# Attention and routed experts on one core: the early tiles' Newton steps on GpSimd, and four operations of the hand-over placed later

## The chip, the cores and the metric

One core of one Trainium2 chip runs the whole program. The metric is the device time of one execution in microseconds, the median over the runs shown. Less is better. Engines are named as in the profile: PE is TensorE, PEld its weight loads, DVE is VectorE, ACT is ScalarE, POOL is GpSimd, SP is SyncE, which here issues most of the transfers.

## The reference

All in float32, for 32 batches of 64 tokens of 512 features (2048 tokens, 16 tiles of 128):

```python
x = x + tanh(g_xattn) * attention(layernorm(x), ctx)       # 32 heads of 128, 4 key/value heads, 128 keys
x = x + tanh(g_ffn) * ffn(layernorm(x))
# ffn, with xt the 2048 normed tokens:
scores = softmax(xt @ router_w + router_b) + router_bias   # 16 experts in 4 groups
# keep the best 2 groups by their maximum, then the best 2 experts; gate = their scores
y = sum over experts of gate * ((silu(xt @ w1 + b1) * (xt @ w2 + b2)) @ w3 + b3)
z = (silu(xt @ sw1 + sb1) * (xt @ sw2 + sb2)) @ sw3 + sb3  # the shared expert, inner width 256
return y + z
```

The layernorm divides by the square root of variance + 1e-5.

## The kernel before, in words

Precision: nearly every product is done as three passes over operands split into a rounded part and a rest (`three_pass`, L82 to L86): hi times hi, lo times hi, hi times lo. So each operand of TensorE is first copied by ScalarE (the hi part) and then subtracted by VectorE (the lo part). `y` in SBUF holds all 16 tiles of the running x.

Stage one makes keys and values. Stage two (`stage_two`) is the attention. It runs 128 steps m (a batch of one key/value head each), and each engine walks the same steps in its own function `step` (ScalarE L810, VectorE L901, TensorE L1036). The order on each engine is written out by hand; semaphores connect them. In step m TensorE makes the scores `ps_s`, turns the previous step's probabilities (`ps_p`), projects queries for a later step (`ps_q`, not in the last four steps), multiplies the probabilities with the values (`ps_o`, which needs VectorE's `p_lo`), and does half of an output product into the one bank `ps_y` (heads 4 to 7 in even steps, 0 to 3 in odd ones, L1012). ScalarE copies half of the scores out (`s_cross`), VectorE adds the other half (`s_sb`, L908), takes the maximum (`nmax`), splits the turned probabilities (`p_lo`), and so on. Every second step VectorE adds a finished tile from `ps_y` into `y` (`add_pair`, L888), and before the next output product starts anew in `ps_y` TensorE waits for that addition (`added`). In the step after an addition VectorE takes the tile's statistics (`moments`, L894). Three more steps (128 to 130) drain the pipeline.

The second norm, its transposes and the router (`SecondNorm`) start inside the last steps. Tiles 0 to 8 are round 0, tiles 9 to 11 round 1, tiles 12 to 15 round 2. For rounds 0 and 1, `inverse_root` (L524 to L541) runs on VectorE at the end of steps 120 and 125: one addition of epsilon, a shift and a subtraction for the first guess, then three Newton iterations of four instructions, each waiting for the one before. Round 2 uses ScalarE's square root after the last addition (L1642). GpSimd norms tiles 0 to 11 and 15 (`normalise`, L561), VectorE tiles 12 to 14. TensorE turns the normed tiles in steps 124 to 128 (`turn`, L574: two, three, three, three, one tile) and the last four after the drain; ScalarE and VectorE split the result into `x_hi` (L582) and `x_lo` (L587). `logits(pe, o, ...)` (L599, L601) makes the router's products of octet o (four tiles, 512 tokens), `copy_logits` (L608) copies them out, and `turn_logits` (L613) turns them to tokens on partitions.

The hooks `act_extra`, `dve_extra` and `pe_extra` (L1466 to L1500) put further operations at the end of a given step: the split of the first shared half's weights (ScalarE step 125, L1120; VectorE step 126, L1155), the copy of the logits of octets 0 and 1 (steps 129, 130) and the router products of octets 0 and 1 (steps 128, 129).

After the drain the routing follows: a chain on VectorE from the logits (L1780) to the choice of experts (`mask`, L1812), then ranks on TensorE (L1968, L1970), slots, and the gathered expert work. The bias rows of the experts (`bias_rows`, `b3`, L1765 and L1768) are split between the last x_lo and the routing. In the trace the tiles `hot_row`/`b` of these lines are `b3_raw` and `b3`, and `w_raw<-bank` and `rows_in<-bank` at L608 are the logits' copies. The last output product of step 130 is followed on TensorE by octet 2's router products, the turned logits of octets 0 and 1, the turns of tiles 12 to 15, octet 3's products, and the first shared half's up products.

Of the kernel before, what the change touches and what calls it, by code (L numbers as in the profile page):

```python
# [22 lines left out]
ACT = mybir.ActivationFunctionType  # L23
# [462 lines left out]
class SecondNorm:  # L486
# [5 lines left out]
    def __init__(self, b, common, signals, normed, x_hi, x_lo, rw, logits_t, roots, banks, fold, bias_copied):  # L492
# [19 lines left out]
        self.roots_made = 0  # L512
# [6 lines left out]
    def inverse_root(self, dve, k):  # L519
# [4 lines left out]
        def then(ins):  # L524
            self.roots_made += 1
            ins.then_inc(self.rooted, 1)
            dve.wait_ge(self.rooted, self.roots_made)

        whole = mybir.dt.uint32
        then(dve.tensor_scalar(v, self.mean_var[:, lo:hi, 1], EPS, None, ALU.add))  # L530
        then(dve.tensor_scalar(w.bitcast(whole), v.bitcast(whole), 1, None, ALU.logical_shift_right))
        then(dve.tensor_scalar(r.bitcast(whole), w.bitcast(whole), -1.0, float(0x5f3759df), ALU.mult, ALU.add))
        for i in range(3):
            then(dve.tensor_tensor(w, r, r, ALU.mult))
            then(dve.tensor_tensor(w, w, v, ALU.mult))
            then(dve.tensor_scalar(w, w, -0.5, 1.5, ALU.mult, ALU.add))
            out = self.rstd[:, lo:hi] if i == 2 else r
            last = dve.tensor_tensor(out, r, w, ALU.mult)  # L538
            if i < 2:
                then(last)  # L540
        last.then_inc(self.rstd_made, 1)  # L541

# [75 lines left out]
def stage_two(nc, a, common, scratch):  # L618
# [4 lines left out]
    with ExitStack() as stack:  # L623
# [236 lines left out]
        def vector(dve):  # L860
# [40 lines left out]
            def step(s, o, g):  # L901
# [41 lines left out]
                if isinstance(s.t, int) and m in (120, 125):  # L943
# [3 lines left out]
                    last.then_inc(front.aggregated, 1)  # L947
                    dve.wait_ge(front.aggregated, m // 125 + 1)
                    front.inverse_root(dve, m // 125)
# [286 lines left out]
def stage_three(nc, a, common, scratch, out):  # L1236
# [12 lines left out]
    with ExitStack() as stack:  # L1249
# [217 lines left out]
        def act_extra(act, m):  # L1467
# [3 lines left out]
            if m == 125:  # L1471
                shared[0].act_split(act, sw_raw[0])
            if m == 128:
                act.wait_ge(consts_made, 1)
                act.activation(spare[:], eps[:], ACT.Sqrt)
            if m in (129, 130):
                front.copy_logits(act, m - 129)

        def dve_extra(dve, m):
# [6 lines left out]
            if m == 126:  # L1486
                shared[0].dve_split(dve, sw_raw[0])

        def pe_extra(pe, m):
# [3 lines left out]
            if m in (128, 129):  # L1493
                front.logits(pe, m - 128, small_lo_made)
# [53 lines left out]
        def _(pool):  # L1548
# [18 lines left out]
            for n in range(12):  # L1567
                front.normalise(pool, n)
# [69 lines left out]
        def _(act):  # L1638
            scalar_two(act)
            act.wait_ge(front.aggregated, 3)  # L1640
# [5 lines left out]
            front.copy_logits(act, 3)  # L1646
            for i in range(2):
# [6 lines left out]
            act.wait_ge(logits_made, 2)  # L1654
            act.activation(probs[:], marks[:], ACT.Exp).then_inc(exp_made, 1)
            act.wait_ge(consts_made, CONSTS)
            act.activation(earlier_r[:], earlier[:], ACT.Copy).then_inc(small_hi_made, 1)
# [461 lines left out]
```

## Time and profile before

| what | value |
|---|---|
| runs, us | 1571.03, 1567.15, 1565.0; median 1567.15 |
| profiled execution | 1573.2 us, its span 1571.4 us |
| busy share of the span | PE 95%, PEld 84%, DVE 63%, ACT 49%, POOL 11% |
| chain that ended last, by engine | PE 65%, issue 7%, DVE 6%, ACT 4% |
| granted TensorE clock | tenths of full speed, 9 in all slices but two of 8 |

The busy share is an average. The part that the change touches lies between 1168 and 1270 us, so it is read there by windows, the timeline of each engine, and the idle times with what ended them. A bracket at the end of a timeline row gives the engine's idle time before the instruction and its releaser. A row of the windows gives the stretch and its length, then the busy time and the number of instructions of PE, PEld, DVE, ACT and POOL, then TensorE's mean granted clock as a share of full speed, the transfers' busy share and GB/s. Rows of one kind that follow each other are merged: their time is that of all together.

### The profile page before, as it was taken

The page shows a single profiled execution, that of the slowest core. Times are in us where ns is not written, and L with a number is a line of the kernel's source. Part 1 is how long each engine was busy: PE and PEld are TensorE (multiplying, and loading weights), DVE is VectorE, ACT ScalarE, POOL GpSimd, SP SyncE. Part 2 cuts the span into 40 slices and gives each one's busy share as a digit, 9 for nine tenths or more (in the row PEclk, how much of TensorE's full clock was granted, in tenths as well). Part 3 has the DMA queues.
Part 4 walks back from the last instruction along what each step waited for, and adds up shares of the span by engine and source line. Part 5 has one row for each costly group of instructions (what it writes and reads, how often), then busy time and mean ns, then how long its engine had stood idle before and what let it go on. Part 6 is the DMA issues. An engine that isn't in the chain of part 4 may idle for free.

```text
span 1571.4 us, 26321 instructions
## 1 busy us (share of the span) xinstructions
PE 1485.3 (95%) x9136; PEld 1316.6 (84%) x9136; DVE 987.5 (63%) x1670; ACT 777.0 (49%) x2022; POOL 180.7 (11%) x174
## 2 busy tenths in 40 slices
PE   7999989999999999999999999999998988888895
PEld 5888878999999999899999989999987777777774
DVE  5322237666777666576766667766677588666648
ACT  3112226555556555465555555655555433666650
POOL 0000000000000000000000000000015113766640
PEclk9999999999999999999999999999999989999998
DMA  7576542111232111222211132112102104776437
GB/s 236 159 221 166 142 147 101 48 68 40 87 112 71 44 52 67 68 68 74 92 50 42 53 97 93 68 48 72 43 29 81 55 1 157 249 236 225 124 109 272
DMA packets 97448, 163.68 MB, mean 104 GB/s; under 512 B 12435, under 2 KB 47287, under 8 KB 93258
## 3 DMA queue, kind: packets, MB, share of 16 engines
q1 hardware_dynamic: 87370, 145.62, 28.5%
q0 software_dynamic: 9984, 16.82, 3.3%
q8 instruction: 58, 0.95, 0.2%
q14 instruction: 36, 0.29, 0.1%
HBM read 128.29 MB, written 49.81 MB: 113 GB/s over the span
## 4 chain that ended last, share of the span: by engine, by line
PE 65%; issue 7%; DVE 6%; ACT 4%; DMA 2%; SPq 2%; another core or an unknown queue 1%; ACTq 0%; POOL 0%; POOLq 0%; DVEq 0%
PE ps_q L84 8%; PE ps_q L86 8%; PE ps_q L85 8%; PE ps_y L85 8%; PE ps_y L86 8%; PE ps_y L84 8%; PE ps_s L993 5%; PE ps_p L1033 3%; PE ps_o L84 2%; PE ps_s L995 2%; PE ps_o L86 2%; PE ps_o L85 2%; DMA w_raw<-in_L_ffn_ew 1%; ACT w_hi L1693 1%; DVE y L1934 1%
## 5 line engine op out<-in xcount | busy, mean ns | idle before, releaser
L84 PE MATMUL ps_q<-xt,wq_hi 128*128 128x256 f32 x1024 | 302.7, 296 | 4.4 <-PEq L118 4.4
L86 PE MATMUL ps_q<-xt,wq_hi 128*128 128x256 f32 x1024 | 292.1, 285 | 0.0
L85 PE MATMUL ps_q<-xt,wq_lo 128*128 128x256 f32 x1024 | 292.0, 285 | 0.0
L828 ACT ACTIVATE s_sb<-s_sb,nmax 128x128 f32<-128x128 f32 x512 | 199.8, 392 | 133.7 <-DVE nmax L910 133.7
L908 DVE TENSOR_TENSOR s_sb<-ps_s,s_cross 128x512 f32<-128x512 f32 x128 | 88.5, 691 | 230.5 <-ACT s_cross L817 230.5
L817 ACT ACTIVATE s_cross<-ps_s 128x512 f32<-128x512 f32 x128 | 76.5, 598 | 272.1 <-PE ps_s L995 272.1
L86 PE MATMUL ps_y<-wo_lo,o_hi 128*128 128x512 f32 x512 | 203.3, 397 | 0.0
L85 PE MATMUL ps_y<-wo_hi,o_lo 128*128 128x512 f32 x512 | 203.1, 397 | 0.0
L84 PE MATMUL ps_y<-wo_hi,o_hi 128*128 128x512 f32 x512 | 202.9, 396 | 0.0
L84 PEld LDWEIGHTS ps_q<-xt,wq_hi 128*128 128x128 f32 x1024 | 197.2, 193 | 5.0 <-issue 4.8
L85 PEld LDWEIGHTS ps_q<-xt,wq_lo 128*128 128x128 f32 x1024 | 197.3, 193 | 0.0
L86 PEld LDWEIGHTS ps_q<-xt,wq_hi 128*128 128x128 f32 x1024 | 196.9, 192 | 0.0
L561 POOL TENSOR_SCALAR normed<-y,mean_var,rstd 128x512 f32<-128x512 f32 x13 | 27.7, 2138 | 981.9 <-DVE rstd L538 966.6
L993 PE MATMUL ps_s<-kt,q_hi 128*128 128x256 f32 x512 | 125.9, 323 | 9.3 <-issue 7.3
L84 PEld LDWEIGHTS ps_y<-wo_hi,o_hi 128*128 128x128 f32 x512 | 96.6, 189 | 24.5 <-issue 1.5
L85 PEld LDWEIGHTS ps_y<-wo_hi,o_lo 128*128 128x128 f32 x512 | 97.0, 190 | 23.4
L86 PEld LDWEIGHTS ps_y<-wo_lo,o_hi 128*128 128x128 f32 x512 | 96.4, 188 | 22.7
L995 PE MATMUL ps_s<-kt,q_lo 128*128 128x128 f32 x512 | 115.0, 225 | 0.0
L993 PEld LDWEIGHTS ps_s<-kt,q_hi 128*128 128x128 f32 x512 | 97.2, 190 | 15.9 <-issue 8.1
L995 PEld LDWEIGHTS ps_s<-kt,q_lo 128*128 128x128 f32 x512 | 98.2, 192 | 5.4
L836 ACT ACTIVATE o_hi<-ps_o 128x512 fp32r<-128x512 f32 x128 | 76.9, 601 | 40.1 <-PE ps_o L86 40.1
L828 ACT ACTIVATION_READ_ACCUMULATOR s_sb<-s_sb,nmax 128x1 f32 x512 | 95.9, 187 | 0.0
(264 smaller groups left out, 3232.5 us busy)
## 6 DMA issues: line engine op xcount, KB each, us to landing
xt<-x_scratch SPq DMA_DIRECT2D x32, 1024.0 KB, 4.8
w_raw<-in_L_ffn_ew SPq DMA_DIRECT2D x93, 256.0 KB
v_full<-v_out SPq DMA_DIRECT2D x64, 128.0 KB, 2.6
k_full<-k_out SPq DMA_DIRECT2D x16, 512.0 KB, 2.8
w_raw<-in_L_xattn_Wq SPq DMA_DIRECT2D x16, 512.0 KB, 5.5
kt_raw<-k_full SPq DMA_DIRECT2D x32, 256.0 KB, 2.7
vt_raw<-v_full SPq DMA_DIRECT2D x32, 256.0 KB, 2.7
w_raw<-in_L_xattn_Wo SPq DMA_DIRECT2D x16, 512.0 KB, 3.9
```

Source lines behind the costliest of these rows:

```text
L84: pe.matmul(out, w_hi, x_hi, start=first, stop=False)
L85: pe.matmul(out, w_lo, x_hi, start=False, stop=False)
L86: return pe.matmul(out, w_hi, x_lo, start=False, stop=last)
L561: eng.tensor_scalar(self.normed[n % RING][:], self.y[:, n, :], self.mean_var[:, n, 0:1], self.rstd[:, n:n + 1], ALU.subtract, ALU.mult).th ...
L817: act.activation(s_cross[:], ps_s[:, :, 1], ACT.Copy).then_inc(cross_copied, 1)
L828: last = act.activation(s_sb[:, i], s_sb[:, i], ACT.Exp, bias=nmax[:, i:i + 1], accum_out=sums[:, i:i + 1])
L836: act.activation(o_hi[s.last_parity][:, :, s.last_token], ps_o[:], ACT.Copy).then_inc(o_hi_made, 1)
L908: dve.tensor_tensor(s_sb[:], ps_s[:, :, 0], s_cross[:], ALU.add).then_inc(folded, 1)
L993: pe.matmul(ps_s[:, i], q_hi[quad_parity][:, batch, heads].rearrange("p h t -> p (h t)"), k[:, :, batch], start=True, stop=False)
L995: last = pe.matmul(ps_s[:, i, 0], q_lo[quad_parity][:, batch, heads].rearrange("p h t -> p (h t)"), k[:, 0, batch], start=False, stop=True)
L1033: last = pe.transpose(ps_p[:, i], p_sb[:, i], ident[:])
L1693: act.activation(w_hi[r][:, 0:2], w_raw[r][:, 0:2], ACT.Copy).then_inc(w_up_hi_made, 1)
```

## The change

Five edits:

- `inverse_root` runs on GpSimd: VectorE makes epsilon's addition and the first guess (`root_seed`, three instructions) at the same place as before, and GpSimd runs the twelve Newton instructions before it norms tile 0 (round 0) and tile 9 (round 1).
- The split of the first shared half's weights moves from step 125 (ScalarE) and 126 (VectorE) to steps 128 and 130.
- The router products of octet 1 move on TensorE from the end of step 129's hook, ahead of its output product, to behind step 130's output product. ScalarE's copy of them moves from step 130's hook to the line before the wait for round 2's statistics.
- ScalarE makes the routing's exponential and `earlier_r` first, and then the hi parts of the bias rows.
- VectorE makes the lo parts of the bias rows after the gates, ahead of its wait for the ranks, and not ahead of the routing.

On TensorE, at the end of steps 128 and 129 and after the drain. `bank3<-x_hi1,rw` are the router products of octet 1, `bank2<-x_hi2,rw` those of octet 2, `ps_y` the output products (each row's kind stands many times). Before:

```order
L86 MATMUL ps_y<-wo_lo,o_hi0 128x512
L599 MATMUL bank3<-x_hi1,rw 32x512
L601 MATMUL bank3<-x_lo1,rw 16x512
...
L84 MATMUL ps_y<-wo_hi,o_hi1 128x512
L85 MATMUL ps_y<-wo_hi,o_lo1 128x512
...
L86 MATMUL ps_y<-wo_lo,o_hi1 128x512
L599 MATMUL bank2<-x_hi2,rw 32x512
L601 MATMUL bank2<-x_lo2,rw 16x512
```

With the change:

```order
L86 MATMUL ps_y<-wo_lo,o_hi0 128x512
L84 MATMUL ps_y<-wo_hi,o_hi1 128x512
L85 MATMUL ps_y<-wo_hi,o_lo1 128x512
...
L86 MATMUL ps_y<-wo_lo,o_hi1 128x512
L613 MATMUL bank3<-x_hi1,rw 32x512
L615 MATMUL bank3<-x_lo1,rw 16x512
...
L613 MATMUL bank2<-x_hi2,rw 32x512
L615 MATMUL bank2<-x_lo2,rw 16x512
```

The eight products of octet 1 no longer stand between the output products of steps 128 and 129, but between the last output product and octet 2's.

On VectorE, at the end of step 120. `mean_var<-stats` are the nine aggregations, `s_sb` the fold of step 121. Before:

```order
L899 BN_AGGR mean_var<-stats 128x2 x9
L530 TENSOR_SCALAR std<-mean_var 128x9
L531 TENSOR_SCALAR trial<-std 128x9
L532 TENSOR_SCALAR root<-trial 128x9
L534 TENSOR_TENSOR trial<-root 128x9
L535 TENSOR_TENSOR trial<-trial,std 128x9
L536 TENSOR_SCALAR trial<-trial 128x9
L538 TENSOR_TENSOR root<-root,trial 128x9
...
L538 TENSOR_TENSOR rstd<-root,trial 128x9
L908 TENSOR_TENSOR s_sb<-ps_s,s_cross 128x512
```

With the change:

```order
L913 BN_AGGR mean_var<-stats 128x2 x9
L552 TENSOR_SCALAR std<-mean_var 128x9
L553 TENSOR_SCALAR trial<-std 128x9
L554 TENSOR_SCALAR root<-trial 128x9
L922 TENSOR_TENSOR s_sb<-ps_s,s_cross 128x512
```

The twelve Newton instructions are gone from VectorE, and in the same way twelve of 128x3 after step 125.

On GpSimd, around tile 9 (buffers `normed_0` and `normed_1` hold tiles 8 and 9), with the change:

```order
L575 TENSOR_SCALAR normed_0<-y,mean_var,rstd 128x512
L532 TENSOR_TENSOR trial<-root 128x3
L533 TENSOR_TENSOR trial<-trial,std 128x3
L534 TENSOR_SCALAR trial<-trial 128x3
L536 TENSOR_TENSOR root<-root,trial 128x3
...
L536 TENSOR_TENSOR rstd<-root,trial 128x3
L575 TENSOR_SCALAR normed_1<-y,mean_var,rstd 128x512
L575 TENSOR_SCALAR normed_2<-y,mean_var,rstd 128x512
```

Before, the norm of tile 9 followed that of tile 8 directly.

The diff, cut to its core:

```diff
@@ SecondNorm
-    def inverse_root(self, dve, k):
+    def inverse_root(self, pool, k):
...
         def then(ins):
             self.roots_made += 1
             ins.then_inc(self.rooted, 1)
-            dve.wait_ge(self.rooted, self.roots_made)
-
-        whole = mybir.dt.uint32
-        then(dve.tensor_scalar(v, self.mean_var[:, lo:hi, 1], EPS, None, ALU.add))
-        then(dve.tensor_scalar(w.bitcast(whole), v.bitcast(whole), 1, None, ALU.logical_shift_right))
-        then(dve.tensor_scalar(r.bitcast(whole), w.bitcast(whole), -1.0, float(0x5f3759df), ALU.mult, ALU.add))
+            pool.wait_ge(self.rooted, self.roots_made)
+
+        pool.wait_ge(self.aggregated, k + 1)
         for i in range(3):
-            then(dve.tensor_tensor(w, r, r, ALU.mult))
-            then(dve.tensor_tensor(w, w, v, ALU.mult))
-            then(dve.tensor_scalar(w, w, -0.5, 1.5, ALU.mult, ALU.add))
+            then(pool.tensor_tensor(w, r, r, ALU.mult))
+            then(pool.tensor_tensor(w, w, v, ALU.mult))
+            then(pool.tensor_scalar(w, w, -0.5, 1.5, ALU.mult, ALU.add))
             out = self.rstd[:, lo:hi] if i == 2 else r
-            last = dve.tensor_tensor(out, r, w, ALU.mult)
+            last = pool.tensor_tensor(out, r, w, ALU.mult)
...
+    def root_seed(self, dve, k):
...
+        then(dve.tensor_scalar(v, self.mean_var[:, lo:hi, 1], EPS, None, ALU.add))
+        then(dve.tensor_scalar(w.bitcast(whole), v.bitcast(whole), 1, None, ALU.logical_shift_right))
+        dve.tensor_scalar(r.bitcast(whole), w.bitcast(whole), -1.0, float(0x5f3759df), ALU.mult, ALU.add
+                          ).then_inc(self.aggregated, 1)
@@ VectorE, steps 120 and 125
-                    last.then_inc(front.aggregated, 1)
-                    dve.wait_ge(front.aggregated, m // 125 + 1)
-                    front.inverse_root(dve, m // 125)
+                    front.seeds_made += 1
+                    last.then_inc(front.seeded, 1)
+                    dve.wait_ge(front.seeded, front.seeds_made)
+                    front.root_seed(dve, m // 125)
@@ act_extra
-            if m == 125:
+            if m == 128:
                 shared[0].act_split(act, sw_raw[0])
-            if m == 128:
                 act.wait_ge(consts_made, 1)
                 act.activation(spare[:], eps[:], ACT.Sqrt)
-            if m in (129, 130):
-                front.copy_logits(act, m - 129)
+            if m == 129:
+                front.copy_logits(act, 0)
@@ dve_extra
-            if m == 126:
+            if m == 130:
                 shared[0].dve_split(dve, sw_raw[0])
@@ pe_extra
-            if m in (128, 129):
-                front.logits(pe, m - 128, small_lo_made)
+            if m == 128:
+                front.logits(pe, 0, small_lo_made)
@@ GpSimd
             for n in range(12):
+                if n in (0, 9):
+                    front.inverse_root(pool, n // 9)
                 front.normalise(pool, n)
@@ ScalarE, behind the drain
             scalar_two(act)
+            front.copy_logits(act, 1)
             act.wait_ge(front.aggregated, 3)
...
             front.copy_logits(act, 3)
+            act.wait_ge(logits_made, 2)
+            act.activation(probs[:], marks[:], ACT.Exp).then_inc(exp_made, 1)
+            act.wait_ge(consts_made, CONSTS)
+            act.activation(earlier_r[:], earlier[:], ACT.Copy).then_inc(small_hi_made, 1)
             for i in range(2):
                 act.activation(bias_rows_hi[i][:], bias_rows[i][:], ACT.Copy).then_inc(small_hi_made, 1)
...
             act.activation(b3[32:64], b3_raw, ACT.Copy).then_inc(small_hi_made, 1)
-            act.wait_ge(logits_made, 2)
-            act.activation(probs[:], marks[:], ACT.Exp).then_inc(exp_made, 1)
-            act.wait_ge(consts_made, CONSTS)
-            act.activation(earlier_r[:], earlier[:], ACT.Copy).then_inc(small_hi_made, 1)
@@ VectorE, ahead of the routing
-            for i in range(2):
-                dve.wait_ge(small_hi_made, i + 2)
-                dve.tensor_tensor(bias_rows_lo[i][:], bias_rows[i][:], f32(bias_rows_hi[i][:]),
-                                  ALU.subtract).then_inc(small_lo_made, 1)
-            dve.wait_ge(small_hi_made, 4)
-            dve.tensor_tensor(b3[64:96], b3_raw, f32(b3[0:32]), ALU.subtract).then_inc(small_lo_made, 1)
...
             link(dve.tensor_scalar(choice_gates[:], choice_gates[:], gain[:], None, ALU.mult))
+
+            for i in range(2):
+                dve.wait_ge(small_hi_made, i + 3)
...
+            dve.wait_ge(small_hi_made, 5)
+            dve.tensor_tensor(b3[64:96], b3_raw, f32(b3[0:32]), ALU.subtract).then_inc(small_lo_made, 1)
 
             dve.wait_ge(ranked, 1)
@@ TensorE
             tensor_two(pe)
+            front.logits(pe, 1, small_lo_made)
             front.logits(pe, 2, small_lo_made)
...
-            pe.wait_ge(small_hi_made, 5)
+            pe.wait_ge(small_hi_made, 2)
```

## Rows read from the trace of the kernel before

**Rows 1.** Windows: steps 121, 122, 126, 127, from score product to score product.

```profile
1168.52:1177.14 8.62, 7.93 (x53) 7.00 (x51) 7.61 (x24) 4.33 (x13) 4.16 (x2) 1.00 0.12 46
1177.14:1184.83 7.69, 7.69 (x52) 7.03 (x51) 5.46 (x10) 4.34 (x13) 0.00 (x0) 1.00 0.05 18
...
1207.33:1218.40 11.07, 8.06 (x41) 6.79 (x39) 9.96 (x31) 5.60 (x15) 6.19 (x3) 0.85 0.14 50
1218.40:1225.81 7.41, 6.57 (x41) 5.53 (x40) 6.07 (x10) 4.77 (x14) 0.00 (x0) 1.00 0.10 36
```

**Rows 2.** Timeline of VectorE, step 121: start, duration, engine, line, instruction.

```profile
1169.11 0.17 DVE L534 TENSOR_TENSOR trial<-root 128x9 f32<-128x9 f32 x1
...
1171.46 0.69 DVE L908 TENSOR_TENSOR s_sb<-ps_s,s_cross 128x512 f32<-128x512 f32 x1
```

**Rows 3.** Timeline of ScalarE, steps 121 and 126.

```profile
1169.59 0.60 ACT L817 ACTIVATE s_cross<-ps_s 128x512 f32<-128x512 f32 x1 [2.58 <-PE ps_s L995]
...
1208.40 0.60 ACT L817 ACTIVATE s_cross<-ps_s 128x512 f32<-128x512 f32 x1 [0.24 <-PE ps_s L995]
```

**Rows 4.** Timeline of VectorE, steps 125 and 126.

```profile
1208.93 0.16 DVE L534 TENSOR_TENSOR trial<-root 128x3 f32<-128x3 f32 x1
...
1211.19 0.69 DVE L908 TENSOR_TENSOR s_sb<-ps_s,s_cross 128x512 f32<-128x512 f32 x1
...
1217.54 1.75 DVE L1155 TENSOR_TENSOR sw_lo<-w_raw,sw_hi 128x1536 fp32r<-128x1536 f32 x1
```

**Rows 5.** Timeline of TensorE, steps 126 and 127.

```profile
1213.26 0.50 PE L84 MATMUL ps_o<-p_hi,vt 128*128 128x512 f32 x1 [3.01 <-DVE p_lo L913]
...
1215.33 0.63 PE L85 MATMUL ps_y<-wo_hi,o_lo 128*128 128x512 f32 x1
...
1219.72 1.60 PE L574 MATMUL bank<-ident,normed 128*128 128x128 f32 x12
1222.16 0.50 PE L84 MATMUL ps_o<-p_hi,vt 128*128 128x512 f32 x1 [0.84 <-DVE p_lo L913]
```

**Rows 6.** Timeline of TensorE, step 129 and the turns after the drain.

```profile
1232.07 0.39 PE L599 MATMUL bank<-x_hi,rw 128*32 128x512 f32 x1
...
1233.93 0.40 PE L84 MATMUL ps_y<-wo_hi,o_hi 128*128 128x512 f32 x1
...
1243.37 1.71 PE L574 MATMUL bank<-ident,normed 128*128 128x128 f32 x12
```

**Rows 7.** Timeline of VectorE, the drain.

```profile
1232.28 0.75 DVE L888 SCALAR_TENSOR_TENSOR y<-ps_y,gain_attn,y 128x512 f32<-128x512 f32 x1 [0.88 <-PE ps_y L86]
...
1239.75 0.75 DVE L888 SCALAR_TENSOR_TENSOR y<-ps_y,gain_attn,y 128x512 f32<-128x512 f32 x1 [5.99 <-PE ps_y L86]
...
1242.19 1.83 DVE L561 TENSOR_SCALAR normed<-y,mean_var,rstd 128x512 f32<-128x512 f32 x3
```

**Rows 8.** Timeline of ScalarE, the root of round 2.

```profile
1241.54 0.30 ACT L1642 ACTIVATE std<-mean_var,eps 128x4 f32<-128x4 f32 x1 [6.83 <-DVE mean_var L899]
```

**Rows 9.** Timeline of TensorE, the last turned logits.

```profile
1251.61 1.06 PE L613 MATMUL bank<-fold,rows_in 32*128 32x16 f32 x8
```

**Rows 10.** Timeline of VectorE, the start of the routing and the wait for the ranks.

```profile
1252.73 0.42 DVE L1780 TENSOR_TENSOR logits<-bank,rb 128x256 f32<-128x256 f32 x1
...
1268.50 0.29 DVE L1821 TENSOR_TENSOR ties<-bank,thresholds 128x128 f32<-128x128 f32 x1 [1.14 <-PE bank L1970]
```

**Rows 11.** Timeline of GpSimd: tiles 9 to 11, a small instruction, two products.

```profile
1211.47 6.19 POOL L561 TENSOR_SCALAR normed<-y,mean_var,rstd 128x512 f32<-128x512 f32 x3 [7.21 <-DVE rstd L538]
...
1244.82 0.23 POOL L1576 TENSOR_SCALAR_AFFINE_SELECT lower<-lower 128x16 f32<-128x16 f32 x1
...
1278.85 3.29 POOL L1557 TENSOR_TENSOR stacked<-rows_in,stacked 32x512 fp32r<-32x512 f32 x2 [30.09 <-ACT rows_in L1665]
```

**Rows 12.** Timeline of VectorE: one product beside GpSimd's, one alone.

```profile
1279.34 1.64 DVE L1851 TENSOR_TENSOR hot_col<-hot_col,token_numbers 128x496 f32<-128x496 f32 x1
...
1289.66 0.68 DVE L1851 TENSOR_TENSOR hot_col<-hot_col,token_numbers 128x496 f32<-128x496 f32 x1
```

More of the change, by code:

```diff
@@ L511, in __init__ @@
         self.logits_turned = b.sem("logits_turned")
-        self.roots_made = 0
+        self.seeded = b.sem("seeded3")
+        self.roots_made = self.seeds_made = 0
     def tiles_in(self, s):
@@ L541, in inverse_root, with then @@
         last.then_inc(self.rstd_made, 1)
+    def root_seed(self, dve, k):
+        lo, hi = self.ROUNDS[k]
+        v, r, w = self.std[:, lo:hi], self.root[:, lo:hi], self.trial[:, lo:hi]
+        whole = mybir.dt.uint32
+        def then(ins):
+            self.seeds_made += 1
+            ins.then_inc(self.seeded, 1)
+            dve.wait_ge(self.seeded, self.seeds_made)
+        then(dve.tensor_scalar(v, self.mean_var[:, lo:hi, 1], EPS, None, ALU.add))
+        then(dve.tensor_scalar(w.bitcast(whole), v.bitcast(whole), 1, None, ALU.logical_shift_right))
+        dve.tensor_scalar(r.bitcast(whole), w.bitcast(whole), -1.0, float(0x5f3759df), ALU.mult, ALU.add
+                          ).then_inc(self.aggregated, 1)
     def wait_normed(self, eng, n):
@@ L1818, in _ @@
             link(dve.tensor_scalar(choice_gates[:], choice_gates[:], gain[:], None, ALU.mult))
+            for i in range(2):
+                dve.wait_ge(small_hi_made, i + 3)
+                dve.tensor_tensor(bias_rows_lo[i][:], bias_rows[i][:], f32(bias_rows_hi[i][:]),
+                                  ALU.subtract).then_inc(small_lo_made, 1)
+            dve.wait_ge(small_hi_made, 5)
+            dve.tensor_tensor(b3[64:96], b3_raw, f32(b3[0:32]), ALU.subtract).then_inc(small_lo_made, 1)
             dve.wait_ge(ranked, 1)
```

## The prediction

> **What bounds the kernel now.** I read the page first: TensorE is busy for nearly the whole span and leads the chain that ended last, so what counts is where TensorE stands still or runs at a lower clock. All edits lie between two places, the end of the attention stage (steps 120 to 130 of the step loop) and the routing that follows it, so I cut this part of the trace into steps at the first score product of each. In the windows [rows 1] an ordinary step takes 7.69 us with TensorE busy throughout. Step 121 takes 8.62 us, and step 126 takes 11.07 us with the granted clock down to 0.85, against 7.41 us for step 127, which has the same make-up (scores, turns of three normed tiles, one output product, no queries). Both long steps follow directly on the two Newton iterations that VectorE runs for the early tiles' inverse roots.
>
> **Round 0, nine tiles, after step 120.** VectorE starts the first Newton product at 1169.11 and reaches the fold of step 121 (s_sb) at 1171.46 [rows 2]. The other operand of that fold, ScalarE's copy s_cross, is done at 1169.59 + 0.60 = 1170.19 [rows 3]. So the twelve Newton instructions hold the fold back by about 1.25 us. The change leaves nine aggregations and three seed instructions on VectorE, which end before 1169.11, so the fold will wait for ScalarE alone, as in any step. TensorE's own work absorbs some of the 1.25 us; what is left is the difference of the step lengths, 8.62 - 7.69 = 0.93 us [rows 1]. **Term: -0.93 us.**
>
> **Round 1, three tiles, after step 125.** The first Newton product starts at 1208.93 and the fold of step 126 at 1211.19 [rows 4]; s_cross was done at 1208.40 + 0.60 = 1209.00 [rows 3]. The fold can start 2.16 us sooner. TensorE waits 3.01 us for p_lo in this step and 0.84 us in step 127 [rows 5]: 3.01 - 2.16 = 0.85, so step 126 should become a second step 127. There is more than the wait in it: 2 us after it TensorE's output products last 0.63 us [rows 5], against 0.40 in the drain [rows 6], with the granted clock of the step at 0.85; the 0.84 us idle of step 127 costs no clock [rows 1, 5]. In the granted clock's two levels this is a stretch at 1.2 GHz after an idle time, inside work at 2.4 GHz. The whole of it is in the difference of the steps, 11.07 - 7.41 = 3.66 us, 2.16 us of wait and 1.5 us of clock. **Term: -3.66 us.**
>
> The shared weights' low part, 1.75 us on VectorE at 1217.54 [rows 4], has to leave this step for that: with the step 3.66 us shorter step 127 starts at 1218.40 - 3.66 = 1214.74, its fold is due 1.7 us later (as 1209.03 stands to 1207.33 in step 126, [rows 1, 3]), at 1216.4, while VectorE, 2.16 us ahead, would be at the split until 1217.54 + 1.75 - 2.16 = 1217.1. The change moves it behind the second last addition into y, where VectorE idles for 5.99 us before the last one [rows 7]. ScalarE's half (three times the 512 elements of a 0.60 us copy, [rows 3], so at most 1.8 us) goes to the drain too, where ScalarE idles 6.83 us before the root [rows 8]. Both cost nothing; the first shared product comes only after the last tiles' turns. Were that cover gone, 1.75 us would stand in front of the last addition.
>
> **The second octet's router products.** These eight products stood between the output products of steps 128 and 129, from 1232.07 to 1233.93 [rows 6], 1.86 us. Removing them doesn't bring the next output product forward by 1.86 us, because it writes the bank from which VectorE adds tile 14 into y, at 1232.28 for 0.75 us [rows 7]. TensorE will stand from 1232.07 to about 1233.1, and the last output product ends only 0.83 us sooner. The eight products come back at full price behind the last output product, in front of the third octet's and the turns of the logits. There TensorE is the engine that decides: it starts the turns of tiles 12 to 14 at 1243.37 with no idle time before them [rows 6], and VectorE had begun to make those tiles at 1242.19 [rows 7]. ScalarE's copy of these logits (about 0.6 us) now stands before the root of the last tiles, so their norm starts about 0.7 us later against the end of the output products, but the turns come 1.86 us later, so TensorE stays the bound. 1.86 - 0.83 = 1.03 us. **Term: +1.03 us**, and it is a loss: the products filled a hole that has nothing else in it. If TensorE were not the bound here, the term would lie between -0.83 + 0.7 = -0.1 and +1.03; I take the upper end, since no idle time is shown before the turns.
>
> **Bias rows later.** The splits stood ahead of the routing's first operation, which adds the router bias to the turned logits. TensorE's last turns of the logits end at 1251.61 + 1.06 = 1252.67 [rows 9], and that operation starts at 1252.73 [rows 10]: without the splits it could start 0.06 us sooner at most. Their new place on VectorE has 1.14 us of waiting for the ranks before 1268.50 [rows 10]; one split of 512 elements at 0.68 us [rows 12] and two of a quarter of that fill it, about 1.1 us. ScalarE's part (two copies of 512 elements at 0.60 us and two small ones, some 1.7 us) goes behind the exponential, and what follows it there is the shared half's activation, for which TensorE has no need until after the ranks. **Term: 0** (from -0.1 to +0.1).
>
> **What GpSimd takes on.** Twelve dependent instructions a round. In round 0 nothing waits: the tiles are turned in step 124, over 20 us later. In round 1 GpSimd begins at about 1209.05 and must still norm tiles 9 and 10 (6.19 / 3 = 2.06 us each [rows 11]) before TensorE turns tile 10. Those twelve turns start at 1219.72 [rows 5]; tile 10 is the last third of 1.60 us, at about 1220.8, and 3.66 us sooner in the new time, at 1217.1. That leaves 1217.1 - 1209.05 - 4.12 = 3.9 us for twelve instructions, and as TensorE waits 0.84 us for p_lo behind the turns anyway [rows 5], 4.8 us before it costs anything: 0.40 us apiece. The trace has no GpSimd product of 128x3. The ends are 12 x 0.20 = 2.4 us (VectorE's own spacing, [rows 2]: 2.35 / 12) and 12 x 1.65 = 19.8 us (GpSimd's TENSOR_TENSOR of 512 elements, 3.29 us for two [rows 11]). The nearest row is the AFFINE_SELECT of 128x16, 0.23 us [rows 11]; with some 0.06 us for the handover, as TensorE takes for that of p_lo, that is 12 x 0.29 = 3.5 us. It fits. **Term: 0**; at the far end it would be 15.0 us of wait and 1.5 us of clock.
>
> The sum: -0.93 - 3.66 + 1.03 = **-3.6 us**. The profiled execution took 1573.2 us and would become 1569.6. The median of the runs is 6.05 us lower, 1567.15; the terms are waits inside one chain that every execution walks, so I set them against the median: **1563.6 us**.
>
> A page that speaks against moving this work: GpSimd's tensor operation and VectorE's do get in each other's way here. A VectorE product of two SBUF operands took 1.64 us while GpSimd ran its TENSOR_TENSORs, and 0.68 us without them [rows 11, 12]. The Trainium skill (GPSIMD Engine Reference, section 1, Specifications) says that GpSimd's SBUF interface is shared with VectorE, with contention for VectorE instructions in a two-port mode or with two SBUF inputs. By that rule the fold and p_lo, which have one operand in PSUM, and the maximum, which has one operand, are left alone, and the sum stays -3.6; the trace agrees as far as it shows such a meeting at all.
>
> **Rivals.**
> (a) *GpSimd's small products are dearer than 0.40 us.* For it: GpSimd needs 2.06 us where VectorE needs 0.6 for a norm, and the far end above. Against it: 0.23 us for the nearest small one. At 0.6 us each (7.2 us) TensorE waits 2.4 us more in step 127; with a stretch of low clock after it, up to 3.9 us. Time 1566 to 1567.5. Chance 0.14, with a tail at the far end (1580) of 0.02.
> (b) *VectorE is held while GpSimd runs Newton*, whatever its operands. Fold, maximum and p_lo, each 512 elements and so about 0.68 us [rows 12], lie wholly in both Newton stretches; stretched by 1.64 / 0.68 = 2.4 they take 2.9 us more in each round, all of it on the path. Step 126 then idles 0.84 + 2.9 us and loses the clock again. -3.6 + 5.8 + 1.5 = +3.7: 1570.9, **slower than before**. It decides from 1.8 us of hold a round upward. Chance 0.05.
> (c) *The drain costs nothing*, since the hole was wider than I think or the products' end did not set the turns: -4.6 us, 1562.5. Chance 0.12.
> (d) *The clock gives nothing back or gives more*: the low stretch moves to another place, such as the 1 us hole of the drain, so the change is worth 1 to 2 us (1565.5), or the stretches behind the later waits go too, another 3 to 6 us. Chance 0.12 and 0.05.
>
> **How the numbers follow.** The forecast has 0.50, and what is near it on both sides (a) to (d). All but the far ends lie within 0.5% (7.8 us), which is about what a measurement of this kernel can tell from no change: faster 0.07 (the upper half of d and luck of the runs), slower 0.03 (the tail of a, the top of b), same 0.90. The runs before lie from 1565.0 to 1571.03, so a median of such runs is itself loose by some 2 us; the range takes in (a) to (c) and this: 1558.5 to 1569.5.
>
> **What would show it.** Right: step 121 at about 7.7 us and step 126 at 7.4 us, the granted clock 1.00 in it; TensorE idle about 1 us before the output product of step 129 with VectorE's y as releaser; the turns of tile 12 following the logits' turns with no idle time; GpSimd's twelve instructions under 4.8 us from first to last. Wrong: an idle time of TensorE before or in the turns of tiles 8 to 10 released by GpSimd (a), folds or maxima longer than 0.7 us during Newton (b), an idle time before the turns of tile 12 (c), a low clock somewhere in steps 121 to 130 (d). From the start of step 120 to the mask of the routing the span should shrink by 3.6 us, with the rest unchanged.

## The result and the profile after

| what | before | after |
|---|---|---|
| median, us (20 runs each) | 1567.32 | 1563.64 |
| lowest to highest | 1563.07 to 1571.47 | 1560.52 to 1568.12 |
| span of the profiled execution | 1571.4 | 1561.6 |
| last p_lo of step 120 to `mask` | 100.79 | 97.31 |

The ratio is 0.9976, with an interval of 0.9966 to 0.9986: 3.7 us less. The interval leaves out 1, but the gain is smaller than the 0.5% that the prediction calls no change. The profiled spans differ by 9.8 us. Only 3.48 us of that lies where the change is. I measure this in the last row of the table: from VectorE's p_lo of step 120 (1163.85 before, 1162.46 after) to its write of `mask` (1264.64 and 1259.77). From `mask` to the routing's slot tokens it is 33.14 and 33.08 us. The rest lies behind the slot tokens, in the expert loop and the tail, whose instructions are the same in both (4.9 us), and ahead of step 120, where nothing was changed (1.4 us). It is no effect of the change that I can show.

The page of the kernel after, its span, busy time and chain:

```profile
span 1561.6 us, 26321 instructions
...
PE 1480.0 (95%) x9136; PEld 1311.9 (84%) x9136; DVE 984.3 (63%) x1646; ACT 777.0 (50%) x2022; POOL 186.8 (12%) x198
...
PE 66%; issue 6%; DVE 6%; ACT 3%; DMA 2%; SPq 2%; another core or an unknown queue 1%; ACTq 0%; POOL 0%; POOLq 0%; DVEq 0%
```

VectorE has 24 instructions fewer than before (1670), GpSimd 24 more (174). The windows of the same four steps, with the columns of [rows 1]:

```profile
1167.11:1174.82 7.71, 7.71 (x53) 7.03 (x52) 5.89 (x12) 4.35 (x13) 5.97 (x14) 1.00 0.07 27
1174.82:1182.50 7.68, 7.68 (x52) 7.02 (x51) 5.31 (x9) 4.35 (x13) 0.65 (x1) 1.00 0.12 44
...
1205.00:1212.39 7.39, 6.55 (x40) 5.66 (x39) 6.55 (x17) 4.77 (x14) 4.63 (x13) 1.00 0.02 4
1212.39:1219.78 7.39, 6.79 (x40) 5.61 (x39) 5.90 (x11) 4.78 (x14) 4.43 (x3) 1.00 0.28 106
```

Step 121 is now like step 122, and step 126 like step 127, with the granted clock back at 1.00, the 2.4 GHz level, where [rows 1] has 0.85. The timeline of GpSimd after, both rounds:

```profile
1167.83 0.20 POOL L532 TENSOR_TENSOR trial<-root 128x9 f32<-128x9 f32 x1 [955.84 <-DVE root L554]
...
1171.00 0.20 POOL L536 TENSOR_TENSOR rstd<-root,trial 128x9 f32<-128x9 f32 x1
...
1206.64 0.19 POOL L532 TENSOR_TENSOR trial<-root 128x3 f32<-128x3 f32 x1 [4.69 <-DVE root L554]
1206.91 0.20 POOL L533 TENSOR_TENSOR trial<-trial,std 128x3 f32<-128x3 f32 x1
...
1209.69 0.20 POOL L536 TENSOR_TENSOR rstd<-root,trial 128x3 f32<-128x3 f32 x1
1210.09 6.73 POOL L575 TENSOR_SCALAR normed<-y,mean_var,rstd 128x512 f32<-128x512 f32 x3 [0.21 <-POOL rstd L536]
```

From the first to the end of the last, round 1 takes 1209.69 + 0.20 - 1206.64 = 3.25 us, 0.27 us apiece: 0.20 of work and 0.07 of handover. The three norms behind it took 6.73 us, where [rows 11] has 6.19: they began at 1210.09, 0.04 us behind VectorE's p_sb, and met it (more on this at the end). The timeline of VectorE after:

```profile
1168.81 0.69 DVE L922 TENSOR_TENSOR s_sb<-ps_s,s_cross 128x512 f32<-128x512 f32 x1 [1.14 <-ACT s_cross L831]
...
1206.70 0.69 DVE L922 TENSOR_TENSOR s_sb<-ps_s,s_cross 128x512 f32<-128x512 f32 x1 [0.15 <-ACT s_cross L831]
...
1226.25 0.75 DVE L902 SCALAR_TENSOR_TENSOR y<-ps_y,gain_attn,y 128x512 f32<-128x512 f32 x1 [0.88 <-PE ps_y L86]
...
1227.65 1.74 DVE L1170 TENSOR_TENSOR sw_lo<-w_raw,sw_hi 128x1536 fp32r<-128x1536 f32 x1
1233.04 0.75 DVE L902 SCALAR_TENSOR_TENSOR y<-ps_y,gain_attn,y 128x512 f32<-128x512 f32 x1 [3.65 <-PE ps_y L86]
...
1247.86 0.42 DVE L1790 TENSOR_TENSOR logits<-bank,rb 128x256 f32<-128x256 f32 x1 [5.01 <-PE bank L627]
...
1263.05 0.68 DVE L1835 TENSOR_TENSOR b<-hot_row,b 32x512 fp32r<-32x512 f32 x1
1263.77 0.29 DVE L1838 TENSOR_TENSOR ties<-bank,thresholds 128x128 f32<-128x128 f32 x1
```

Both folds (s_sb) now wait for ScalarE's s_cross, not for Newton [rows 2, 4]; the weights' split (sw_lo) sits in the idle time before the last addition (5.99 us in [rows 7], 3.65 left); and the bias rows sit in the wait for the ranks, which is gone without a remainder ([rows 10] had 1.14 us of it). The timeline of TensorE after:

```profile
1208.77 0.50 PE L84 MATMUL ps_o<-p_hi,vt 128*128 128x512 f32 x1 [0.84 <-DVE p_lo L927]
...
1216.15 0.51 PE L84 MATMUL ps_o<-p_hi,vt 128*128 128x512 f32 x1 [0.60 <-DVE p_lo L927]
...
1227.15 0.47 PE L84 MATMUL ps_y<-wo_hi,o_hi 128*128 128x512 f32 x1 [0.94 <-DVE y L902]
...
1232.84 0.40 PE L613 MATMUL bank<-x_hi,rw 128*32 128x512 f32 x1
...
1236.63 1.95 PE L627 MATMUL bank<-fold,w_raw 32*128 32x16 f32 x16
1238.52 1.71 PE L588 MATMUL bank<-ident,normed 128*128 128x128 f32 x12
```

The wait of 3.01 us in [rows 5] is 0.84 us. The hole of the drain is there (0.94 us, released by VectorE's y), and the turns of tiles 12 to 14 follow the turned logits with no idle time.

### The profile page after: what moved, and what is told of

Read it like the earlier page. It is cut to its first block, busy times and chain, and to the rows that moved or that the text cites. A ratio compares the mean times of both kernels' runs of the same rounds, so it can differ in the third digit from the quotient of the medians.

```text
span 1561.6 us, 26321 instructions
## 1 busy us (share of the span) xinstructions
PE 1480.0 (95%) x9136; PEld 1311.9 (84%) x9136; DVE 984.3 (63%) x1646; ACT 777.0 (50%) x2022; POOL 186.8 (12%) x198
## 4 chain that ended last, share of the span: by engine, by line
PE 66%; issue 6%; DVE 6%; ACT 3%; DMA 2%; SPq 2%; another core or an unknown queue 1%; ACTq 0%; POOL 0%; POOLq 0%; DVEq 0%
PE ps_q L84 8%; PE ps_q L86 8%; PE ps_q L85 8%; PE ps_y L85 8%; PE ps_y L84 8%; PE ps_y L86 8%; PE ps_s L1008 5%; PE ps_p L1048 4%; PE ps_o L84 2%; PE ps_s L1010 2%; PE ps_o L86 2%; PE ps_o L85 2%; DMA w_raw<-in_L_ffn_ew 1%; DVE y L1951 1%; DVE y L1205 1%
```

## The experiments

Each job's runs of the kernel before were made on its own chip: their medians were 1557.3, 1558.1 and 1558.0 us in the three jobs, 10 us below those of the result, so only ratios within a job and stretches of a trace are compared. "The stretch" is that from p_lo of step 120 to `mask`. The diffs are against the changed kernel. The first four runs shared one job.

**e1: only Newton moved.** The four other edits are undone.

```diff
-            if m == 128:
+            if m == 125:
                 shared[0].act_split(act, sw_raw[0])
-            if m == 130:
+            if m == 126:
                 shared[0].dve_split(dve, sw_raw[0])
-            if m == 128:
-                front.logits(pe, 0, small_lo_made)
+            if m in (128, 129):
+                front.logits(pe, m - 128, small_lo_made)
```

> The kernel before with the Newton iterations on GpSimd and nothing else changed. Measured from the p_lo of step 120 to the choice mask (100.79 us before, 97.31 us with the whole change). My theory (Newton pays, the drain's move costs, the shared split costs a part of step 127 if it stays): 0.93 + 3.66 us gained, some 0.7 us of it lost again to the split of the shared weights in step 126, no loss in the drain: 96.9 us, so it beats the whole change by 0.4 us; total 3.9 us under before. Rival (the other three edits carry part of the gain): 98 us or more.

Measured: 1552.85 us, ratio 0.9966 (0.9953 to 0.9979); the stretch 97.01 us. The folds of steps 125, 126 and 127 stand 7.39 and 8.27 us apart (7.41 and 7.39 in the changed kernel), so the split costs 0.88 us where it stood. The timelines of VectorE in e1:

```profile
1215.03 2.00 DVE L1170 TENSOR_TENSOR sw_lo<-w_raw,sw_hi 128x1536 fp32r<-128x1536 f32 x1
1216.95 0.68 DVE L922 TENSOR_TENSOR s_sb<-ps_s,s_cross 128x512 f32<-128x512 f32 x1
```

and of TensorE:

```profile
1219.00 0.51 PE L84 MATMUL ps_o<-p_hi,vt 128*128 128x512 f32 x1 [1.48 <-DVE p_lo L927]
```

The fold starts as the split ends, and TensorE waits 1.48 us, not 0.60. The split itself took 2.00 us here beside GpSimd's norms, 1.75 in [rows 4]. Moving Newton is the whole gain, and moving the split protects 0.88 us of it; with nothing but Newton moved the stretch is 0.3 us shorter than with the whole change (97.31), because the drain's loss is not in it.

**e2: the second octet's products back in step 129.**

```diff
-            if m == 129:
-                front.copy_logits(act, 0)
+            if m in (129, 130):
+                front.copy_logits(act, m - 129)
-            if m == 128:
-                front.logits(pe, 0, small_lo_made)
+            if m in (128, 129):
+                front.logits(pe, m - 128, small_lo_made)
...
-            front.copy_logits(act, 1)
...
-            front.logits(pe, 1, small_lo_made)
```

> The whole change, but the second octet's router products again between the output products of steps 128 and 129. Theory: they fill the time in which TensorE waits for VectorE's addition; the stretch to the mask falls from 97.31 to 96.1 us, the total 1.2 us under the changed kernel. Rival (what stands before the turns is not TensorE's work but the last tiles' norm, or the copy of the logits): the stretch stays at 97.3.

Measured: 1550.49 us, ratio 0.9951 (0.9936 to 0.9965); the stretch 96.06 us, last addition to logits 12.94. Against the changed kernel the stretch is 1.25 us shorter, as the drain's term has it. The median is lower than that term alone makes it; e9 and e10 come back to this.

**e3: Newton back on VectorE, the rest of the change kept.**

```diff
                     front.root_seed(dve, m // 125)
+                    if m // 125 in (0, 1):
+                        front.inverse_root(dve, m // 125)
```

(and the call on GpSimd left out)

> The whole change, but the Newton iterations on VectorE again, directly after the seeds. Theory: step 121 at 8.6 us, step 126 at 11.1 us with 3.0 us of TensorE's wait and the granted clock at 0.85; the stretch to the mask rises by 4.6 us to 101.9, a little slower than before (by 1.1 us). Rival (the low clock of step 126 did not come from the wait): step 126 at 9.6 us, the stretch at 100.4.

Measured: 1558.15 us, ratio 1.0005 (0.9992 to 1.0017); the stretch 102.51 us. The timeline of TensorE in step 126 of e3:

```profile
1210.94 0.51 PE L84 MATMUL ps_o<-p_hi,vt 128*128 128x512 f32 x1 [3.01 <-DVE p_lo L927]
...
1212.21 0.57 PE L86 MATMUL ps_y<-wo_lo,o_hi 128*128 128x512 f32 x1
1212.58 0.63 PE L84 MATMUL ps_y<-wo_hi,o_hi 128*128 128x512 f32 x1
```

The wait of 3.01 us and the products at 0.63 us come back together, to the hundredth as in [rows 5]: both belong to Newton's place. Step 121 is 8.63 us again, and step 126 11.08 us with the granted clock at 0.85. Without it the other four edits are worth nothing or a small loss: the stretch is 1.7 us longer than before (100.79), 1.2 us of which is the drain. 0.6 us of the stretch is more than expected; it is the turns of the last tiles and the first shared up products, which ran at the 1.2 GHz level.

**e4: beyond the change, shared products ahead of the wait for the mask.** e2's kernel, with this:

```diff
+            pe.wait_ge(shared[0].gate_copied, 1)
+            shared[0].pe_up_part(pe, 2, 0, 0, C)
             pe.wait_ge(mask_made, 1)
...
-            shared[0].pe_up(pe, 2, True)
+            shared[0].pe_up_part(pe, 2, 1, 0, C)
```

> As e2, and in the routing TensorE makes the first half of the third octet's shared up products (12 products) ahead of its wait for the mask, not behind the ranks. Theory: TensorE's wait of 3.2 us for the mask becomes about 0.4, the low clock behind it goes, and VectorE's wait of 4.2 us for the first one-hot products shrinks to near nothing: about 4 us less between the mask and the third hot_row (20.56 us before), total 5.2 us under the changed kernel. Rival (VectorE and GpSimd slow each other there and are the bound): under 2 us.

Measured: 1550.6 us, ratio 0.9952 (0.9938 to 0.9966): nothing over e2 in the median. TensorE's wait for the mask (3.16 us in the kernel after, 1.59 in e2) is gone. From `mask` to the slot tokens it is 30.72 us, against 31.43 in e2 and 33.08 in the kernel after. The shared half's results come sooner, and so do GpSimd's products on them, which meet VectorE's one-hot products (hot_row, hot_col). The timeline of VectorE in e4:

```profile
1268.43 2.04 DVE L1862 TENSOR_TENSOR hot_row<-lanes,lane 128x1024 f32<-128x1024 f32 x1 [0.20 <-DVE lane L1852]
1270.38 1.76 DVE L1863 TENSOR_TENSOR hot_col<-columns,column 128x496 f32<-128x496 f32 x1
...
1273.48 1.22 DVE L1862 TENSOR_TENSOR hot_row<-lanes,lane 128x1024 f32<-128x1024 f32 x1
1274.62 1.74 DVE L1863 TENSOR_TENSOR hot_col<-columns,column 128x496 f32<-128x496 f32 x1
1276.39 1.62 DVE L1865 TENSOR_TENSOR hot_col<-hot_col,choice_gates 128x496 f32<-128x496 f32 x1
```

and of GpSimd:

```profile
1268.10 1.27 POOL L1571 TENSOR_TENSOR stacked<-rows_in,stacked 32x512 fp32r<-32x512 f32 x1 [24.63 <-ACT rows_in L1681]
1269.78 1.83 POOL L1571 TENSOR_TENSOR stacked<-rows_in,stacked 32x512 fp32r<-32x512 f32 x1 [0.41 <-ACT rows_in L1681]
1274.54 1.29 POOL L1571 TENSOR_TENSOR stacked<-rows_in,stacked 32x512 fp32r<-32x512 f32 x1 [2.93 <-ACT rows_in L1681]
1276.22 1.25 POOL L1571 TENSOR_TENSOR stacked<-rows_in,stacked 32x512 fp32r<-32x512 f32 x1 [0.40 <-ACT rows_in L1681]
```

Such meetings are not new, as the timeline of VectorE in e2 shows:

```profile
1270.15 2.32 DVE L1862 TENSOR_TENSOR hot_row<-lanes,lane 128x1024 f32<-128x1024 f32 x1
1272.39 1.75 DVE L1863 TENSOR_TENSOR hot_col<-columns,column 128x496 f32<-128x496 f32 x1
...
1276.83 2.06 DVE L1862 TENSOR_TENSOR hot_row<-lanes,lane 128x1024 f32<-128x1024 f32 x1 [1.26 <-PE bank L2007]
1278.81 1.73 DVE L1863 TENSOR_TENSOR hot_col<-columns,column 128x496 f32<-128x496 f32 x1
```

Alone these VectorE products take 1.22 and 0.68 us. The meetings cost (2.04 - 1.22) + (1.76 - 0.68) + (1.74 - 0.68) + (1.62 - 0.68) = 3.9 us in e4, and (2.32 - 1.22) + (1.75 - 0.68) + (2.06 - 1.22) + (1.73 - 0.68) = 4.1 us in e2. What changed is where they fall: all four now stand ahead of the third hot_row, where e2 has two of them and 1.26 us of waiting for TensorE (the kernel after 3.13). VectorE's own chain fills the time that the shorter wait left, and the third hot_row starts 19.33 us after the mask, in e2 18.95, in the kernel after 20.56. That fits the rival of this run (VectorE and GpSimd are the bound there): 1.2 us less than in the kernel after, where 4 were expected. Behind the third hot_row e4 is 1.1 us shorter than e2, which makes the 0.7 us to the slot tokens; why the median doesn't show even that stays open.

**e5: six Newton iterations on GpSimd, not three** (`range(6)`; this job also has e6 to e8). It doubles the suspected cost. The results of the extra iterations are the same roots.

> The whole change with six Newton iterations a round in place of three (twice the work on GpSimd; the root has converged, so its values stay). The changed kernel's trace has 0.28 us from one of GpSimd's Newton instructions to the next, so 24 of them take 6.6 us in round 1. Theory (4.8 us are free): tile 10 comes 2.0 us too late for TensorE even after the wait for p_lo is used up, step 127 grows by 2.0 us, by 3.5 if the clock falls behind it; the stretch from p_lo of step 120 to the mask is 99.3 to 100.8 us against 97.31. In round 0 the longer Newton lies under p_sb of step 121, which has two SBUF operands: by the row of the hot_col product it is stretched from 0.69 to 1 us or more. Rival (GpSimd's work is hidden whatever its length, the tiles come long before their turn): 97.3.

Measured: 1554.51 us in one run; the stretch 99.53 us, 2.2 us more than the whole change. The timeline of TensorE in e5, step 127:

```profile
1216.46 0.75 PE L588 MATMUL bank<-ident,normed 128*128 128x128 f32 x4 [1.55 <-POOL normed L575]
...
1218.52 0.75 PE L588 MATMUL bank<-ident,normed 128*128 128x128 f32 x4 [1.32 <-POOL normed L575]
```

That is rival (a) as it would have looked: the turns of tiles 9 and 10 wait for GpSimd, 2.87 us in all, less the 0.60 us of the p_lo wait behind them. GpSimd's 24 instructions of the round last 6.9 us (1207.22 to 1214.12), 2.1 us over the 4.8 that the prediction had to spend, and that is what it costs. The other half of what I expected here did not come: VectorE's p_sb, a product of two SBUF operands that now meets GpSimd's, is not stretched. The timeline of GpSimd in round 0 of e5:

```profile
1173.02 0.53 POOL L532 TENSOR_TENSOR trial<-root 128x9 f32<-128x9 f32 x1
...
1174.77 0.62 POOL L533 TENSOR_TENSOR trial<-trial,std 128x9 f32<-128x9 f32 x1
```

and of VectorE:

```profile
1172.78 0.72 DVE L941 TENSOR_TENSOR p_sb<-s_sb,rsums 128x512 f32<-128x512 f32 x1
...
1174.65 0.68 DVE L891 TENSOR_TENSOR kt<-kt_raw,kt 128x512 fp32r<-128x512 f32 x1
```

It is GpSimd that is held: its 0.20 us products last until VectorE's end (1173.55 beside 1173.50; 1175.39 beside 1175.33).

**e6: four iterations** (`range(4)`), a small step on the same scale.

> The whole change with four Newton iterations a round, 16 instructions, 4.4 us in round 1. Theory: under the 4.8 us that are free, so the stretch to the mask stays at 97.3 us (within 0.2). Rival (there is no slack; each iteration is paid): 98.4.

Measured: 1553.98 us in one run; the stretch 97.31 us, the whole change's own. The turn of tile 10 waits 0.94 us for GpSimd, the wait for p_lo behind it is gone, and the additions into y come 0.08 us later, counted from the start of step 127. The sixteen instructions last 4.69 us (1208.05 to 1212.74), not the 4.4 expected, since one of them met p_sb and took 0.56 us; that is just under 4.8. Four more a round are free, twelve more are not.

**e7: e2's kernel with the bias rows ahead of the routing again.**

```diff
-            act.wait_ge(logits_made, 2)
-            act.activation(probs[:], marks[:], ACT.Exp).then_inc(exp_made, 1)
...
+            for i in range(2):
+                dve.wait_ge(small_hi_made, i + 2)
```

> As e2 (octet 1's products back in their hole), but the bias rows of the experts split ahead of the routing, as before. Theory: the last addition to the first routing operation stays at 12.9 us within 0.1 and the wait for the ranks is free again, so the place of the bias rows is worth nothing either way, and the stretch to the mask is 96.1. Rival (moving them paid some of the gain): 0.5 us or more longer.

Measured: 1554.52 us in one run; the stretch 96.13 us against 96.06, last addition to logits 12.98 against 12.94. The bias rows cost 0.04 us where they stood, if anything.

**e8: the whole change, beside e5 to e7.**

> The whole change as it is, to have it beside the kernel before in the same job as the others: 3.7 us under before, ratio 0.9976, the stretch to the mask 97.3 us; e2 was 0.9951, so 1.2 us or more should lie between them.

Measured: 1554.97 us, ratio 0.9977 (0.9967 to 0.9988); the stretch 98.17 us.

**e9 and e10: e2's kernel and the whole change once more, on one chip.**

> Once more the whole change with octet 1's router products left in the hole of step 129, now on the same chip and beside the same runs as the whole change (e10). If only the stretch between steps 120 and the mask differs, e9's time lies 1.2 us (the drain's term, 1.18) below e10's, and the ratio to before is about 0.9969. If the placement also moves low-clock products out of the routing, e9 lies 3 to 4 us below e10, ratio about 0.9952, as e2 and e8 had it on two chips. From p_lo of step 120 to the mask: 96.1 us; last addition to logits 12.9 us.

> The whole change once more beside e9. Ratio to before 0.9977 as in both comparisons so far; from p_lo of step 120 to the mask 97.3 us, or up to 98.3 where low-clock products fall into the first shared up products; last addition to logits 14.8 us or more.

Measured: e9 1551.71 us, ratio 0.9955 (0.9942 to 0.9968), the stretch 97.01 us; e10 1555.71 us, ratio 0.9987 (0.9970 to 1.0003), the stretch 98.16 us. The interval of e10 just reaches 1. The kernel with the placement in the hole is faster beside the whole change on one chip, by 4.0 us between the medians, and 1.15 us of it is shown to be the placement's, in the stretch. The timeline of TensorE behind the turns of the last tile, in e10:

```profile
1241.34 1.10 PE L588 MATMUL bank<-ident,normed 128*128 128x128 f32 x4 [0.38 <-DVE x_lo L601]
1242.09 0.78 PE L84 MATMUL bank<-x_hi,sw_hi 128*128 128x512 f32 x1
1242.67 0.63 PE L85 MATMUL bank<-x_hi,sw_lo 128*128 128x512 f32 x1
```

and in the kernel after, the same program:

```profile
1240.77 0.72 PE L588 MATMUL bank<-ident,normed 128*128 128x128 f32 x4 [0.55 <-DVE x_lo L601]
1241.25 0.48 PE L84 MATMUL bank<-x_hi,sw_hi 128*128 128x512 f32 x1
1241.56 0.39 PE L85 MATMUL bank<-x_hi,sw_lo 128*128 128x512 f32 x1
```

In e8, e9 and e10 turns and a few products run here at the 1.2 GHz level (0.63 us), and not in the result's own execution: 0.9 us in the stretch. No long wait stands before it: the twelve turns ahead of the wait of 0.38 us are already slower (1.88 us in e10, 1.71 in the kernel after). In these three `mask` to slot tokens is also 34.25 us, not 33.1 (in e2 31.4). One execution of one kernel can therefore be off by a us or two against another. e9 and e10 have this alike, so it does not explain the other 2.85 us between their medians. In their profiled executions e9 is also 3.5 us ahead at step 120, where both programs are the same, and its expert loop is 1.9 us shorter; my second rival, fewer low-clock products in the routing, shows in e2 and not in e9. That rest stays open.

**e11: e9's kernel with round 0 alone back on VectorE.**

> e9's kernel with the Newton iterations of round 0 alone back on VectorE (round 1 stays on GpSimd). If the two rounds are independent, as the sum has it, the fold of step 121 is 0.9 us later and nothing else moves: from p_lo of step 120 to the mask 96.1 + 0.9 = 97.0 us, steps 126 and 127 at 7.4 us each, granted clock 1.00 in both. Rival: round 0's wait is absorbed in the 40 us behind it (p_lo waits of steps 122 to 125), then 96.1 us.

Measured: 1556.54 us in one run; the stretch 97.03 us where e2 had 96.06; steps 126 and 127 at 7.39 and 7.36 us between folds. Beside e9, which differs by round 0 alone and ran in the same job, the whole stretch shows nothing (97.01), because e9 has the 0.9 us of low clock behind its last addition and e11 has not (last addition to logits 13.82 and 12.96 us). Up to the last addition into y, which that doesn't touch, it is 72.16 us in e11, 71.28 in e9 and 71.22 in e2. The round's 0.9 us is there, and nothing later absorbs it.

## Why the prediction was right, point by point

- **Round 0, -0.93 us.** Step 121 went from 8.62 to 7.71 us, and e11 brings 0.9 us back. Right.
- **Round 1, -3.66 us.** Step 126 went from 11.07 to 7.39 us (-3.68), and its granted clock from 0.85 to 1.00. e3 brings the wait and the low clock back together. That 1.5 us of the gain were clock was right; rival (d) did not come true there.
- **The shared weights' split, 0.** Free in the drain. Left where it was it would have cost 0.88 us (e1); the working (1217.1 against 1216.4) gave 0.7. It left out that the split grows beside GpSimd's norms.
- **The second octet's products, +1.03 us.** The mechanism was right, hole and turns both; the size was off by 0.15. The last addition came 0.68 us sooner, not 0.83, because the hole holds 0.94 us idle and the first product behind it starts slower (0.47 us against 0.40). 1.86 - 0.68 = 1.18 us, and e2 gives back 1.25. Rival (c), a free drain, is out.
- **Bias rows, 0.** 0.04 us at the old place (e7). At the new one they fill the wait for the ranks exactly: the b row ends at 1263.73, and the next operation, at 1263.77, waits for nothing.
- **GpSimd's Newton, 0.** 0.27 us apiece, where I took 0.29 and had 0.40 to spend. The working left out that the norms behind Newton can grow: they took 6.73 us, not 6.19, tile 10 was ready 0.2 us late for its turn (the turns of step 127 last 1.84 us, not 1.60), and the wait for p_lo, down to 0.60 us, took that in. e6 (four iterations, free) and e5 (six, 2.2 us) enclose the bound of 4.8 us: the working of the slack stands, and the term is 0. Rival (a) needed 0.40.
- **Rival (b), VectorE held.** No fold, maximum or p_lo is longer than 0.69 us. The page's rule (Trainium skill, GPSIMD Engine Reference, section 1, Specifications) names VectorE instructions in a two-port mode or with two SBUF inputs, and so spares these; here the trace agrees. It would also have allowed a longer p_sb in e5, which did not come (0.72 us): GpSimd's product was the one that was held.
- **The sum.** -0.93 - 3.66 + 1.18 = -3.4 us; the stretch measured -3.48, the median of the result -3.7. e8 and e10 gave -3.1 and -2.3 by their medians. The mechanism was right, but that the result's median met the forecast of 1563.6 us to 0.1 us is luck: the stretch of this same program is 0.9 us longer in e8 and e10.

## What to carry to other kernels

Count a wait together with what the clock does behind it: of the 3.66 us in round 1, 2.16 were the wait. Before you move products that "only" sit between others, look for the wait that they cover: they come back at full price if another engine sets the next start. And when GpSimd is given work, look not at its duration alone but at which VectorE products with two SBUF operands it will meet, which of the two will have started first, and whether GpSimd's instruction is itself a product of two tensors.

## What the runs showed of the hardware

- **GpSimd and VectorE take turns on products of two SBUF operands.** In e4 GpSimd had started first four times, and VectorE's product then ended most of its own time after GpSimd's: 1274.62 + 1.74 = 1276.36, 0.53 us after 1275.83; 1276.39 + 1.62 = 1278.01, 0.54 us after 1277.47; 1270.38 + 1.76 = 1272.14, 0.53 us after 1271.61; 1268.43 + 2.04 = 1270.47, 1.10 us after 1269.37. Once it is the other way round: GpSimd's product of 1269.78 lasts 1.83 us and ends 1.14 us after VectorE's hot_row. In e5 VectorE had started first, and GpSimd's 0.20 us products end 0.05 us after VectorE's. So the price of a meeting is about what is left of the product that the other has begun: 0.8 to 1.1 us for VectorE beside GpSimd's products of 1.3 us, and 0.03 us beside those of 0.2 us (p_sb in e5). The Trainium skill (Trainium Architecture — The Big Picture, section What this means for kernel authors) calls this port pair "an exclusive lock (not a bandwidth split)"; these rows agree.
- **A norm on GpSimd does not hold VectorE in this way.** The norm reads one tensor, with two scalars per partition. In the kernel before, p_sb began inside GpSimd's second norm (three from 1211.47 on, 2.06 us each [rows 11]) and was not lengthened:

```profile
1214.54 0.69 DVE L927 TENSOR_TENSOR p_sb<-s_sb,rsums 128x512 f32<-128x512 f32 x1
```

If whoever starts first kept a lock, p_sb would have waited about 1 us. In e1 the weights' split, beside such norms from start to end, grew by 0.25 us. The other direction is there: where p_sb had started first, the three norms took 6.73 us (kernel after). So who waits is not settled by who started first alone; whether the number of tensors that GpSimd reads decides was not tested.
- **No fixed factor.** The prediction's rival (b) reckoned with a factor of 2.4 on every operation of VectorE; folds, maxima and p_lo beside GpSimd's Newton took 0.68 to 0.69 us.
- **Small products are cheap on GpSimd.** 128x3 and 128x9 both take 0.19 to 0.21 us, unless they meet VectorE (0.53 to 0.62), as against 0.17 on VectorE [rows 2], while a norm of 512 elements takes 2.1 us against 0.6.
- **Idle time and clock.** 3.01 us of idle time in step 126 were followed by the 1.2 GHz level in both kernels that had it (before, e3); 1.55 and 1.32 us, with turns between them, were not (e5), nor were 1.48 us (e1). In e8 to e10 the level fell in turns with no wait of more than 1 us near them. So the length of the wait alone doesn't tell here whether the clock falls.
